# Second score products that begin with the row of maxima and end with the masks, on a TensorE that drops waits it has already made

## The chip, the cores and the metric

The kernel runs on 1 core of one Trainium2 chip. The metric is the device time in microseconds (us) of one execution. The kernel before takes 1175.02 us, the median of three runs (1172.75, 1175.02 and 1177.32).

## The reference

Everything is 32-bit. `x` is 4 sequences of 1024 tokens of width 128.

```
x = x + layernorm(attention(layernorm(x)))
x = x + layernorm(ffn(layernorm(x)))

attention(x): xn = layernorm(x) * g + b
    q, k, v = xn @ wq + bq, xn @ wk + bk, xn @ wv + bv      (16 heads of 64)
    scores = q @ k.T / 8;  scores[key < query] = -inf       (a query sees itself and what follows)
    out = softmax(scores) @ v @ w0 + b0 + x
ffn(x): down and up projections of 8 experts of rank 16, gated by the top 2 of the
    first token's logits
```

The inputs are drawn so that scores are large; a score must be right to nearly full 32-bit precision.

## The kernel before, in words

The work is cut into 32 slots of one pair of heads each (`t`, 4 sequences x 8 pairs), and each engine's program is written out slot by slot. A head has 64 rows, so every product of the pair is issued twice, head `h` on rows 0 to 63 and 64 to 127 of the array; the two run side by side, and a step of the array means such a pair here.

Scores are made twice. The **first** products, `score(n, s)` (S0 to S8, lines 519 to 529), have queries on partitions; they are single products `q_high x k_high`, and VectorE takes each row's maximum from them (L895, L890). GpSimd and a transpose (`m`) turn the maxima into the row `shift_row` of two bf16 parts. The **second** products, `score_t(n, s)` (T0 to T9, lines 531 to 558), have keys on partitions. Each tile of them is a sum in one PSUM bank per head of: three products of 32-bit operands (fp32r: `k_high x q_low`, `k_low x q_high`, `k_high x q_high`, L549), the row of maxima spread over the keys (`pick x shift_row`, bf16, L552), and, on the diagonal, four short bf16 products of 128 columns that add the mask (`mask_half x ident_half`, L556; in S tiles L527). ScalarE then takes the exponentials (L760) into `total` (T0 and T7) or a `ring` of five tiles. `weigh(n, s)` multiplies them with `v` (L571), and GpSimd adds them up (L417) for the sums of the softmax, which `sum_up` (L581) reduces over the partitions in the next slot.

A slot has three groups, each a string of S (first products of the slot ahead) and T (second products), then fills (`q`, `k`, `v` projections, L494 to L496 and L510 to L512, `out` L593, `sum` L581, `m` L587), then `weigh`:

```
ORDER = ["STTSTS", "STTSTTS", "STTSTS"]
T_STEPS = [range(0, 3), range(3, 7), range(7, 10)]
S_STEPS = [(1, range(3, 6)), (1, range(6, 9)), (2, range(0, 3))]
```

So TensorE's row is S3 T0 T1 S4 T2 S5, fills, weigh; S6 T3 T4 S7 T5 T6 S8, fill, weigh; S0 T7 T8 S1 T9 S2, fills, weigh. Masks end S1, S3, S6, S7, S8 and T4 to T9; T6 and T9 are two blocks each, of 384 and 128 columns, both with masks. T0 to T3 have none. T5 and T8 have 256 columns, the others 512.

Two PSUM banks, `st0` and `st1`, hold the T tiles in turn: T(s) waits for the exponential of T(s-2) (`s_exp`). There is one bank `s_ps` for the S tiles, so each S waits until VectorE has the maxima of the one before (`s_max`). Waits on TensorE are written where they are needed (`wait_ge`, `reach`, `wait_taken`), also where an earlier instruction of TensorE has already waited for the same or a later count.

Of the kernel before, what the change touches and what calls it, by code (L numbers as in the profile page):

```python
# [5 lines left out]
def sandwich_kernel(nc, x, ln_gb, w_pairs, qk_bias, bv, w0, b0, router_t, down_t, up_r, out, sums_dram):  # L6
# [102 lines left out]
    with ctx:  # L109
# [360 lines left out]

        @block.tensor
        def _(pe):
            def next_use(use):

                bank, index = USE[use]
                reach(pe, s_free[bank], index)

            def turn_four(src, a, bank=pp):
                for j in range(4):
# [3 lines left out]
            def project(weight, n):  # L483
                b, p = divmod(n, PAIRS)
                if b:
                    wait_taken(pe, "z", b, 0)
                else:
                    pe.wait_ge(s_xlow, 2)
                pe.wait_ge(s_w_low, 1 if p < 2 else 2)
                use = ("qk"[weight], n, 0)  # L490
                high, low = wqk_high[:, p, weight, :], wqk_low[:, p, weight, :]
                for c in range(2):
                    dst, tokens = at(*use)[:, c * HALF:(c + 1) * HALF], slice(c * HALF, (c + 1) * HALF)
                    nc.tensor.matmul(dst, high, x_low[:, tokens], start=True, stop=False)  # L494
                    nc.tensor.matmul(dst, low, x_high[:, tokens], start=False, stop=False)  # L495
                    last = nc.tensor.matmul(dst, high, x_high[:, tokens], start=False, stop=True)  # L496
                return last

            def project_v(n, part):
                b, p = divmod(2 * n, PAIRS)  # L500
                if b:
                    wait_taken(pe, "z", b, 0)
                else:
                    pe.wait_ge(s_xlow, 2)
                pe.wait_ge(s_w_low, 1 if p < 2 else 2)
                high, low = (w[:, p:p + 2, :].rearrange("p a c -> p (a c)") for w in (wv_high, wv_low))
                for a in range(4):
                    t = 4 * part + a
                    dst, tokens = at("v", n, part)[:, a * 2 * P:(a + 1) * 2 * P], slice(t * P, (t + 1) * P)
                    nc.tensor.matmul(dst, x_low[:, tokens], high, start=True, stop=False)  # L510
                    nc.tensor.matmul(dst, x_high[:, tokens], low, start=False, stop=False)
                    last = nc.tensor.matmul(dst, x_high[:, tokens], high, start=False, stop=True)  # L512
                return last

            def score(n, s):

                if s == 0:
                    pe.wait_ge(s_high, 2 * n + 2)
                reach(pe, s_max, BLOCK_STEPS * n + s)
                rows = [slice(h * D, (h + 1) * D) for h in range(2)]  # L520
                for i, k0, w, col, diagonal in BLOCKS[s]:
                    for h in range(2):
                        last = nc.tensor.matmul(s_ps[:, h, col:col + w], q_high[n % 3][rows[h], i * P:(i + 1) * P],  # L523
                                                k_high[n % 3][rows[h], k0:k0 + w], start=True, stop=not diagonal)
                    for a in range(2 * diagonal):
                        for h in range(2):
                            last = nc.tensor.matmul(s_ps[:, h, col:col + P], ident_half[rows[h], a, :],  # L527
                                                    mask_half[rows[h], a, :], start=False, stop=(a == 1))
                last.then_inc(s_score, 1)

            def score_t(n, s):

                half = half_of(s)
                if s == 0:
                    wait_taken(pe, "k", n, 0)
                if s == 0:
                    pe.wait_ge(s_shift_row, 32 * n + 32)
                reach(pe, s_exp, STEPS * n + s - 1)
                g = 0 if s < 3 else 1 if s < 7 else 2
                reach(pe, s_free[s % 2], filled[n, g][s % 2])  # L540
                rows = [slice(h * D, (h + 1) * D) for h in range(2)]
                b = n % 3
                for _, j, w, col in TILES[s]:
                    keys, queries = slice(j * P, (j + 1) * P), slice(half * HALF, half * HALF + w)
                    dst = [st[s % 2][:, h, col:col + w] for h in range(2)]
                    diagonal = j // 4 == half
                    for k, q in ((k_high[b], q_low[b]), (k_low[b], q_high[b]), (k_high[b], q_high[b])):
                        for h in range(2):
                            nc.tensor.matmul(dst[h], k[rows[h], keys], q[rows[h], queries], start=(q is q_low[b]),  # L549
                                             stop=False)  # L550
                    for h in range(2):
                        last = nc.tensor.matmul(dst[h], pick[rows[h], :], shift_row[n % 2][rows[h], queries], start=False,  # L552
                                                stop=not diagonal)
                    for a in range(2 * diagonal):
                        for h in range(2):
                            last = nc.tensor.matmul(dst[h][:, w - P:w], mask_half[rows[h], a, :],  # L556
                                                    ident_half[rows[h], a, :], start=False, stop=(a == 1))
                last.then_inc(s_st, 1)

            def weigh(n, s):  # L560

                half = half_of(s)
                pe.wait_ge(s_exp, STEPS * n + s + 1)
                if s in FIRST:
                    reach(pe, s_o, 2 * n + half)
                if s == 0:
                    wait_taken(pe, "v", n // 2, 1)
                for k, (_, j, w, col) in enumerate(TILES[s]):
                    for h in range(2):
                        c0 = (n % 2) * P + h * D  # L570
# [3 lines left out]
                last.then_inc(s_pv, 1)  # L574

            def sum_up(n):
                pe.wait_ge(s_add, SUMS * (n + 1))
                for half in range(2):
                    for h in range(2):
                        g = 2 * half + h  # L580
# [2 lines left out]
                return last  # L583

            def turn_shift(n):
                pe.wait_ge(s_shift, n + 1)
                return nc.tensor.transpose(pp[:].bitcast(bf16)[0:32, 0:P], shift[:].rearrange("p h s i -> p (h s i)"),  # L587
                                           ident_bf[:])

            def project_out(n):  # L590
                pe.wait_ge(s_norm, n + 1)
                for t in range(QB):
                    last = nc.tensor.matmul(at("out", n, 0)[:, t * P:(t + 1) * P], o_norm[:, t * P:(t + 1) * P],  # L593
                                            w0_sb[:, n % PAIRS, :], start=True, stop=True)
# [9 lines left out]
            def fill(use, bank):  # L604
# [11 lines left out]
                elif kind == "out":  # L616
                    last = project_out(n)
                elif kind == "c0":
                    pe.wait_ge(s_bvw, 1)
                    for p in range(PAIRS):  # L620
                        last = nc.tensor.matmul(dst[:, 0:E], bv_wide[:, p, :], w0_sb[:, p, :], start=(p == 0),
                                                stop=(p == PAIRS - 1))
                elif kind == "z":
                    pe.wait_ge(s_z, n + 1)
                    for a in range(2):
                        last = turn_four(z_a, a, dst[:, a * HALF:(a + 1) * HALF])
                elif kind == "u":
                    pe.wait_ge(s_u, n + 1)
                    for a in range(2):
                        last = turn_four(u_b, a, dst[:, a * HALF:(a + 1) * HALF])  # L630
                elif kind == "logit":
                    pe.wait_ge(s_first, n + 1)
                    last = nc.tensor.matmul(dst[:, 0:EXPERTS], first_tok[:], router_sb[:], start=True, stop=True)
                elif kind == "down":
                    wait_taken(pe, "u", n, 0)
                    for a in range(2):
                        half = slice(a * HALF, (a + 1) * HALF)
                        last = nc.tensor.matmul(dst[:, half], down_sb[:], u_t[:, half], start=True, stop=True)
                elif kind == "up":
                    wait_taken(pe, "down", n, 0)  # L640
                    pe.wait_ge(s_upg, n + 1)
                    for a in range(2):
                        last = project_up(dg_t, a, dst[:, a * HALF:(a + 1) * HALF])
                last.then_inc(s_fill[bank], 1)

            pe.wait_ge(s_const, 5)
            pe.wait_ge(s_small, 16 * 8)
            pe.wait_ge(s_z0, 1)
            turn_four(z_a, 0, st[0][:, 0, :]).then_inc(s_zt, 1)
            pe.wait_ge(s_z, 1)  # L650
            turn_four(z_a, 1, st[0][:, 1, :]).then_inc(s_xt, 1)

            for t in SLOTS:
                for g in range(3):
# [7 lines left out]
                            score_t(t, s)  # L662
                    for use, bank in fills(t, g):
                        if bank != "pp" and 0 <= t < N:
                            pe.wait_ge(s_exp, STEPS * t + T_STEPS[g][-1] + (bank == T_STEPS[g][-1] % 2))
                        fill(use, bank)
                    if 0 <= t < N:
                        for s in T_STEPS[g]:
                            weigh(t, s)

            b = B - 1
            pe.wait_ge(s_u, B)
            turn_four(u_b, 0, st[0][:, 0, :])
            turn_four(u_b, 1, st[0][:, 1, :]).then_inc(s_tail, 1)
            pe.wait_ge(s_first, B)
            nc.tensor.matmul(pp[:, 0:EXPERTS], first_tok[:], router_sb[:], start=True, stop=True).then_inc(s_tail, 1)
            pe.wait_ge(s_ut_out, 2)
            for a in range(2):
                last = nc.tensor.matmul(st[1][:, a, :], down_sb[:], u_t[:, a * 512:(a + 1) * 512], start=True, stop=True)
            last.then_inc(s_tail, 1)  # L680
            pe.wait_ge(s_dg, 2)
            pe.wait_ge(s_upg, B)
            for a in range(2):
                last = project_up(dg_t, a, s_ps[:, a, :])
            last.then_inc(s_tail, 1)
# [422 lines left out]
```

## Time and profile before

| | us |
|---|---|
| median of three runs | 1175.02 |
| the profiled execution | 1177.26 |
| its span, first to last instruction | 1175.5 |
| TensorE (PE) busy | 1048.6 (89%) |
| GpSimd (POOL) busy | 746.3 (63%) |
| VectorE (DVE) busy | 546.3 (46%) |
| ScalarE (ACT) busy | 541.7 (46%) |
| granted TensorE clock, mean | 0.957 |

Busy times are unions of an engine's records; PE is the matmuls, PEld the loads of their stationary operand, which may run beside a matmul. A matmul's record includes the time until its result is written, so records of neighbours overlap; the distance from start to start tells what a step costs. A steady slot is 31.2 us long.

### The profile page before, as it was taken

How to read it: one execution, taken by the hardware profiler on the slowest of the kernel's cores; microseconds unless marked ns; L12 is line 12 of the kernel's file. 1: busy time of each engine (PE TensorE's matmuls, PEld its weight loads, DVE VectorE, ACT ScalarE, POOL GpSimd, SP SyncE). 2: the span in 40 equal slices, each digit the busy share in tenths (PEclk: the TensorE clock that was granted, in tenths of full speed). 3: DMA queues.
4: the chain of work that ended last, by engine and by line, in shares of the span. 5: the costliest groups of instructions: out<-in, count | busy, mean ns of one | idle time of the engine just before them, and what ended most of it. 6: DMA issues, size and time to landing. Idle time of an engine off the chain costs nothing.

```text
span 1175.5 us, 22750 instructions
## 1 busy us (share of the span) xinstructions
PE 1048.6 (89%) x9160; PEld 648.2 (55%) x9160; DVE 546.3 (46%) x748; ACT 541.7 (46%) x738; POOL 746.3 (63%) x681
## 2 busy tenths in 40 slices
PE   0679999999999998999999998999999999999513
PEld 0345655665666665666655665666565656655312
DVE  1345455455445544455545554555555545452012
ACT  3124554444444564554454553654454454543212
POOL 8006768666666866765776866766776766765531
PEclk9979999999999998999999998999999999999855
DMA  3000000001001000001002100000002000000010
GB/s 97 0 19 3 20 20 20 20 20 38 20 21 25 19 16 20 20 20 38 20 20 56 20 19 2 21 20 20 20 20 56 20 20 20 12 14 16 19 54 18
DMA packets 63174, 27.62 MB, mean 23 GB/s; under 512 B 40160, under 2 KB 54880, under 8 KB 63072
## 3 DMA queue, kind: packets, MB, share of 16 engines
q1 hardware_dynamic: 63072, 26.18, 9.6%
q8 instruction: 74, 1.21, 0.4%
q14 instruction: 28, 0.23, 0.1%
HBM read 23.28 MB, written 2.36 MB: 22 GB/s over the span
## 4 chain that ended last, share of the span: by engine, by line
PE 74%; POOL 10%; ACT 7%; DVE 5%; issue 3%; DMA 1%; POOLq 0%; SPq 0%; ACTq 0%; DVEq 0%
PE po L571 20%; PE st L549 14%; PE s_ps L523 7%; PE st L593 5%; POOL total L417 5%; PE st L552 4%; PE st L494 4%; DVE least L895 4%; ACT ring L760 3%; PE pp L581 3%; PE st L496 3%; PE st L495 3%; ACT total L760 3%; PE s_ps L527 2%; PE st L510 2%
## 5 line engine op out<-in xcount | busy, mean ns | idle before, releaser
L417 POOL TENSOR_TENSOR total<-total,ring 128x1024 f32<-128x1024 f32 (+3 forms) x320 | 549.2, 1716 | 325.4 <-PE po L571 292.7
L895 DVE TENSOR_REDUCE least<-s_ps 128x2 f32<-128x1024 f32 (+2 forms) x320 | 317.9, 1010 | 316.4 <-PE s_ps L527 207.7
L760 ACT ACTIVATE ring<-st 128x1024 f32<-128x1024 f32 (+1 forms) x256 | 234.8, 918 | 227.0 <-PE st L552 152.7
L571 PE MATMUL po<-ring,v_sb 128*64 128x512 f32 (+3 forms) x1280 | 210.7, 467 | 0.0
L523 PE MATMUL s_ps<-k_high,q_high 64*128 64x512 f32 (+3 forms) x768 | 165.1, 442 | 21.1 <-DVE least L895 15.9
L549 PE MATMUL st<-q_low,k_high 64*128 64x512 f32 (+3 forms) x768 | 168.2, 434 | 5.2 <-ACT total L760 1.1
L571 PEld LDWEIGHTS po<-ring,v_sb 128*64 128x64 f32 x1280 | 89.0, 137 | 135.4 <-issue 125.7
L549 PE MATMUL st<-q_high,k_low 64*128 64x512 f32 (+3 forms) x768 | 133.3, 343 | 0.0
L549 PE MATMUL st<-q_high,k_high 64*128 64x512 f32 (+3 forms) x768 | 133.1, 342 | 0.0
L552 PE MATMUL st<-shift_row,pick 64*128 64x512 bf16 (+3 forms) x768 | 129.6, 333 | 0.0
L523 PEld LDWEIGHTS s_ps<-k_high,q_high 64*128 64x128 f32 x768 | 74.5, 190 | 71.2 <-issue 36.5
L760 ACT ACTIVATE total<-st 128x1024 f32<-128x1024 f32 x64 | 65.6, 1025 | 61.5 <-PE st L552 34.8
L549 PEld LDWEIGHTS st<-q_low,k_high 64*128 64x128 f32 x768 | 73.5, 187 | 29.2 <-ACT total L760 19.8
L424 POOL TENSOR_TENSOR o_norm<-o_raw,inv_row 128x1024 f32<-128x1024 f32 x32 | 75.8, 2368 | 14.7 <-DMA inv_row<-sums_dram 14.7
L942 DVE SCALAR_TENSOR_TENSOR q_low<-st,bias_col,q_high 128x1024 fp32r<-128x1024 f32 x32 | 41.1, 1284 | 85.3 <-ACT q_high L788 85.3
L766 ACT COPY o_raw<-po 128x512 f32<-128x512 f32 x64 | 37.4, 584 | 91.4 <-PE po L571 91.2
L593 PE MATMUL st<-w_sb,o_norm 128*128 128x128 f32 x512 | 67.5, 289 | 11.5 <-POOL o_norm L424 11.4
L549 PEld LDWEIGHTS st<-q_high,k_high 64*128 64x128 f32 x768 | 72.5, 185 | 8.4
L593 PEld LDWEIGHTS st<-w_sb,o_norm 128*128 128x128 f32 x512 | 66.8, 205 | 17.8 <-issue 13.3
L549 PEld LDWEIGHTS st<-q_high,k_low 64*128 64x128 f32 x768 | 73.3, 187 | 2.9
L552 PEld LDWEIGHTS st<-shift_row,pick 64*128 64x128 bf16 x768 | 37.2, 93 | 65.6 <-issue 62.8
L527 PE MATMUL s_ps<-mask_half,ident_half 64*128 64x128 bf16 x1024 | 71.8, 224 | 0.0
(133 smaller groups left out, 1325.9 us busy)
## 6 DMA issues: line engine op xcount, KB each, us to landing
inv_row<-sums_dram SPq DMA_DIRECT2D x64, 256.0 KB, 4.0
x_a<-x SPq DMA_DIRECT2D x4, 512.0 KB, 4.7
sums<-sums_row SPq DMA_DIRECT2D x128, 2.0 KB, 2.1
x_b<-x SPq DMA_DIRECT2D x4, 512.0 KB, 5.7
out<-res_b SPq DMA_DIRECT2D x4, 512.0 KB, 4.1
ring<-w_pairs SPq DMA_DIRECT2D x1, 1152.0 KB, 8.4
shift_row<-shift_t SPq DMA_DIRECT2D x64, 4.0 KB
w_sb<-w SPq DMA_DIRECT2D x1, 512.0 KB, 5.3
```

Source lines behind the costliest of these rows:

```text
L417: nc.gpsimd.tensor_tensor(so_far, so_far, tile_of(n, s)[:, :, col:col + w], ALU.add).then_inc(s_add, 1)
L424: nc.gpsimd.tensor_tensor(o_norm[:], o_raw[n % 2][:], inv_row[:], ALU.mult).then_inc(s_norm, 1)
L494: nc.tensor.matmul(dst, high, x_low[:, tokens], start=True, stop=False)
L523: last = nc.tensor.matmul(s_ps[:, h, col:col + w], q_high[n % 3][rows[h], i * P:(i + 1) * P], k_high[n % 3][rows[h], k0:k0 + w], start=Tru ...
L527: last = nc.tensor.matmul(s_ps[:, h, col:col + P], ident_half[rows[h], a, :], mask_half[rows[h], a, :], start=False, stop=(a == 1))
L549: nc.tensor.matmul(dst[h], k[rows[h], keys], q[rows[h], queries], start=(q is q_low[b]), stop=False)
L552: last = nc.tensor.matmul(dst[h], pick[rows[h], :], shift_row[n % 2][rows[h], queries], start=False, stop=not diagonal)
L571: last = nc.tensor.matmul(po[h * D:(h + 1) * D, 0:w], v_sb[(n // 2) % 2][:, j, c0:c0 + D], tile_of(n, s)[:, h, col:col + w], start=(s in F ...
L593: last = nc.tensor.matmul(at("out", n, 0)[:, t * P:(t + 1) * P], o_norm[:, t * P:(t + 1) * P], w0_sb[:, n % PAIRS, :], start=True, stop=True)
L760: nc.scalar.activation(tile_of(n, s)[:, :, 0:w], st[s % 2][:, :, 0:w], ACT.Exp, scale=SCALE).then_inc(s_exp, 1)
L895: last = nc.vector.tensor_reduce(least[:, :, a:a + 1], s_ps[:, :, col:col + w], AX.X, ALU.max, negate=True)
L942: nc.vector.scalar_tensor_tensor(out=low[n % 3][:], in0=src, scalar=bias_col[:, n % PAIRS, w:w + 1], in1=high[n % 3][:].bitcast(fp32), op0 ...
```

## The change

Two edits, both in TensorE's program. In `score_t`, each tile begins with the row of maxima and then takes its three 32-bit products, the two small ones in the other order; the masks, where there are some, follow the last 32-bit product. And TensorE keeps, per semaphore, the highest count it has waited for (`made`); `need` emits a wait only where the count is higher. All waits of TensorE go through it. Other engines are not touched.

```diff
+            made = {}
+
+            def need(semaphore, count):
+
+                if count > made.get(semaphore, 0):
+                    made[semaphore] = count
+                    pe.wait_ge(semaphore, count)
+
+            def need_taken(*use):
+                bank, index = USE[use]
+                need(s_free[bank], index + 1)
...
-                    for k, q in ((k_high[b], q_low[b]), (k_low[b], q_high[b]), (k_high[b], q_high[b])):
+                    for h in range(2):
+                        nc.tensor.matmul(dst[h], pick[rows[h], :], shift_row[n % 2][rows[h], queries], start=True, stop=False)
+                    for part, (k, q) in enumerate(((k_low[b], q_high[b]), (k_high[b], q_low[b]), (k_high[b], q_high[b]))):
                         for h in range(2):
-                            nc.tensor.matmul(dst[h], k[rows[h], keys], q[rows[h], queries], start=(q is q_low[b]),
-                                             stop=False)
-                    for h in range(2):
-                        last = nc.tensor.matmul(dst[h], pick[rows[h], :], shift_row[n % 2][rows[h], queries], start=False,
-                                                stop=not diagonal)
+                            last = nc.tensor.matmul(dst[h], k[rows[h], keys], q[rows[h], queries], start=False,
+                                                    stop=(part == 2 and not diagonal))
                     for a in range(2 * diagonal):
...
             def weigh(n, s):
 
                 half = half_of(s)
-                pe.wait_ge(s_exp, STEPS * n + s + 1)
+                need(s_exp, STEPS * n + s + 1)
                 if s in FIRST:
-                    reach(pe, s_o, 2 * n + half)
+                    need(s_o, 2 * n + half)
```

Every other `wait_ge`, `reach` and `wait_taken` of TensorE becomes `need` or `need_taken` in the same way. In the built program TensorE's instructions that do nothing but wait go from 749 to 174, and matmuls that carry a wait from 1142 to 883; the 7956 matmuls stay.

TensorE's row in the second group of a slot, where S6 ends and T3 begins, before (names are output<-moving operand, stationary operand; columns of the output at the end):

```order
L523 MATMUL s_ps<-k_high,q_high 128x256 x2
L527 MATMUL s_ps<-mask_half,ident_half 128x128 x4
L549 MATMUL st<-q_low,k_high 128x512 [waits s_free_1,s_exp]
L549 MATMUL st<-q_low,k_high 128x512
L549 MATMUL st<-q_high,k_low 128x512 x2
L549 MATMUL st<-q_high,k_high 128x512 x2
L552 MATMUL st<-shift_row,pick 128x512 x2
```

The same place now:

```order
L535 MATMUL s_ps<-k_high,q_high 128x256 x2
L539 MATMUL s_ps<-mask_half,ident_half 128x128 x4
L560 MATMUL st<-shift_row,pick 128x512 [waits s_free_1]
L560 MATMUL st<-shift_row,pick 128x512
L563 MATMUL st<-q_high,k_low 128x512 x2
L563 MATMUL st<-q_low,k_high 128x512 x2
L563 MATMUL st<-q_high,k_high 128x512 x2
```

A bf16 product now stands behind the bf16 masks, and the wait for `s_exp` is gone from it, since an earlier one covers it.

TensorE's row a little later in the same group, where T6 begins behind T5's masks, before:

```order
L556 MATMUL st<-ident_half,mask_half 128x128 x4
L549 MATMUL st<-q_low,k_high 128x384 [waits s_free_0,s_exp]
L549 MATMUL st<-q_low,k_high 128x384
L549 MATMUL st<-q_high,k_low 128x384 x2
L549 MATMUL st<-q_high,k_high 128x384 x2
L552 MATMUL st<-shift_row,pick 128x384 x2
L556 MATMUL st<-ident_half,mask_half 128x128 x4
```

And now:

```order
L567 MATMUL st<-ident_half,mask_half 128x128 x4
L560 MATMUL st<-shift_row,pick 128x384 [waits s_exp]
L560 MATMUL st<-shift_row,pick 128x384
L563 MATMUL st<-q_high,k_low 128x384 x2
L563 MATMUL st<-q_low,k_high 128x384 x2
L563 MATMUL st<-q_high,k_high 128x384 x2
L567 MATMUL st<-ident_half,mask_half 128x128 x4
```

The wait for the exponential stays and now holds the bf16 product; the masks follow a 32-bit product instead of a bf16 one.

## Rows read from the trace of the kernel before

**Rows 1.** The page: shares of the chain that ended last, by engine.

```profile
PE 74%; POOL 10%; ACT 7%; DVE 5%; issue 3%; DMA 1%; POOLq 0%; SPq 0%; ACTq 0%; DVEq 0%
```

**Rows 2.** The chain in a steady slot: start us, us, engine, output, line.

```profile
605.03 1.03 ACT ring L760
606.07 0.04 issue
606.11 0.79 PE st L549 x6
...
614.57 1.03 ACT total L760
...
615.65 0.79 PE st L549 x6
...
624.55 1.24 DVE least L895
...
637.30 0.80 PE st L549 x6
```

**Rows 3.** Timeline, S6's masks and T3: start us, us, engine, line, operation.

```profile
602.68 0.29 PE L527 MATMUL s_ps<-mask_half,ident_half 64*128 64x128 bf16 x4
...
603.09 0.39 PE L549 MATMUL st<-q_high,k_low 64*128 64x512 f32 x2
...
603.32 0.40 PE L549 MATMUL st<-q_high,k_high 64*128 64x512 f32 x2
...
603.56 0.20 PEld L549 LDWEIGHTS st<-q_low,k_high 64*128 64x128 f32 x2
...
603.79 0.19 PEld L549 LDWEIGHTS st<-q_high,k_low 64*128 64x128 f32 x2
```

**Rows 4.** Timeline, T4's masks, S7, S7's masks, T5.

```profile
604.71 0.28 PE L556 MATMUL st<-ident_half,mask_half 64*128 64x128 bf16 x4
...
604.80 0.48 PE L523 MATMUL s_ps<-k_high,q_high 64*128 64x512 f32 x2
...
605.12 0.29 PE L527 MATMUL s_ps<-mask_half,ident_half 64*128 64x128 bf16 x4
...
605.22 0.36 PE L549 MATMUL st<-q_low,k_high 64*128 64x256 f32 x2
```

**Rows 5.** Timeline, T6 from its wait on: loads and masks.

```profile
606.11 0.19 PEld L549 LDWEIGHTS st<-q_low,k_high 64*128 64x128 f32 x2 [0.23 <-ACT ring L760]
...
606.22 0.19 PEld L549 LDWEIGHTS st<-q_high,k_low 64*128 64x128 f32 x2
...
606.92 0.28 PE L556 MATMUL st<-ident_half,mask_half 64*128 64x128 bf16 x4
606.98 0.19 PEld L549 LDWEIGHTS st<-q_low,k_high 64*128 64x128 f32 x2
...
607.09 0.19 PEld L549 LDWEIGHTS st<-q_high,k_low 64*128 64x128 f32 x2
...
607.37 0.10 PEld L552 LDWEIGHTS st<-shift_row,pick 64*128 64x128 bf16 x2
...
607.38 0.15 PEld L556 LDWEIGHTS st<-ident_half,mask_half 64*128 64x128 bf16 x4
```

**Rows 6.** Timeline, steps of 512 columns before `out`, and before weigh.

```profile
597.32 0.39 PE L496 MATMUL st<-x_high,wqk_high 128*128 128x512 f32 x1
597.55 0.72 PE L593 MATMUL st<-w_sb,o_norm 128*128 128x128 f32 x5
```

**Rows 7.** Timeline, the end of the `k` fill and the first product of weigh.

```profile
609.50 0.40 PE L496 MATMUL st<-x_high,wqk_high 128*128 128x512 f32 x1
609.83 2.37 PE L571 MATMUL po<-ring,v_sb 128*64 128x512 f32 x12
```

**Rows 8.** Waits of TensorE (us, times, longest), and one slot's busy times and clock.

```profile
PE pp L581 <- POOL total L417: 18.0, 4, 8.9
...
723.80:757.90 34.10, 33.80 (x284) 20.70 (x285) 14.05 (x15) 18.39 (x29) 23.19 (x23) 0.91 0.08 18
```

More of the change, by code:

```diff
@@ L472, in _ @@
         def _(pe):
+            made = {}
[6 more added lines that the diff above has]
+                need(s_free[bank], index + 1)
             def next_use(use):
                 bank, index = USE[use]
-                reach(pe, s_free[bank], index)
+                need(s_free[bank], index)
             def turn_four(src, a, bank=pp):
@@ L485, in project @@
                 if b:
-                    wait_taken(pe, "z", b, 0)
+                    need_taken("z", b, 0)
                 else:
-                    pe.wait_ge(s_xlow, 2)
-                pe.wait_ge(s_w_low, 1 if p < 2 else 2)
+                    need(s_xlow, 2)
+                need(s_w_low, 1 if p < 2 else 2)
                 use = ("qk"[weight], n, 0)
@@ L501, in project_v @@
                 if b:
-                    wait_taken(pe, "z", b, 0)
+                    need_taken("z", b, 0)
                 else:
-                    pe.wait_ge(s_xlow, 2)
-                pe.wait_ge(s_w_low, 1 if p < 2 else 2)
+                    need(s_xlow, 2)
+                need(s_w_low, 1 if p < 2 else 2)
                 high, low = (w[:, p:p + 2, :].rearrange("p a c -> p (a c)") for w in (wv_high, wv_low))
@@ L517, in score @@
                 if s == 0:
-                    pe.wait_ge(s_high, 2 * n + 2)
-                reach(pe, s_max, BLOCK_STEPS * n + s)
+                    need(s_high, 2 * n + 2)
+                need(s_max, BLOCK_STEPS * n + s)
                 rows = [slice(h * D, (h + 1) * D) for h in range(2)]
@@ L534, in score_t @@
                 if s == 0:
-                    wait_taken(pe, "k", n, 0)
+                    need_taken("k", n, 0)
                 if s == 0:
-                    pe.wait_ge(s_shift_row, 32 * n + 32)
-                reach(pe, s_exp, STEPS * n + s - 1)
+                    need(s_shift_row, 32 * n + 32)
+                need(s_exp, STEPS * n + s - 1)
                 g = 0 if s < 3 else 1 if s < 7 else 2
-                reach(pe, s_free[s % 2], filled[n, g][s % 2])
+                need(s_free[s % 2], filled[n, g][s % 2])
                 rows = [slice(h * D, (h + 1) * D) for h in range(2)]
@@ L562, in weigh @@
                 half = half_of(s)
-                pe.wait_ge(s_exp, STEPS * n + s + 1)
+                need(s_exp, STEPS * n + s + 1)
                 if s in FIRST:
-                    reach(pe, s_o, 2 * n + half)
+                    need(s_o, 2 * n + half)
                 if s == 0:
-                    wait_taken(pe, "v", n // 2, 1)
+                    need_taken("v", n // 2, 1)
                 for k, (_, j, w, col) in enumerate(TILES[s]):
@@ L576, in sum_up @@
             def sum_up(n):
-                pe.wait_ge(s_add, SUMS * (n + 1))
+                need(s_add, SUMS * (n + 1))
                 for half in range(2):
@@ L585, in turn_shift @@
             def turn_shift(n):
-                pe.wait_ge(s_shift, n + 1)
+                need(s_shift, n + 1)
                 return nc.tensor.transpose(pp[:].bitcast(bf16)[0:32, 0:P], shift[:].rearrange("p h s i -> p (h s i)"),
@@ L590, in project_out @@
             def project_out(n):
-                pe.wait_ge(s_norm, n + 1)
+                need(s_norm, n + 1)
                 for t in range(QB):
@@ L618, in fill @@
                 elif kind == "c0":
-                    pe.wait_ge(s_bvw, 1)
+                    need(s_bvw, 1)
                     for p in range(PAIRS):
@@ L623, in fill @@
                 elif kind == "z":
-                    pe.wait_ge(s_z, n + 1)
+                    need(s_z, n + 1)
                     for a in range(2):
@@ L627, in fill @@
                 elif kind == "u":
-                    pe.wait_ge(s_u, n + 1)
+                    need(s_u, n + 1)
                     for a in range(2):
@@ L631, in fill @@
                 elif kind == "logit":
-                    pe.wait_ge(s_first, n + 1)
+                    need(s_first, n + 1)
                     last = nc.tensor.matmul(dst[:, 0:EXPERTS], first_tok[:], router_sb[:], start=True, stop=True)
                 elif kind == "down":
-                    wait_taken(pe, "u", n, 0)
+                    need_taken("u", n, 0)
                     for a in range(2):
@@ L639, in fill @@
                 elif kind == "up":
-                    wait_taken(pe, "down", n, 0)
-                    pe.wait_ge(s_upg, n + 1)
+                    need_taken("down", n, 0)
+                    need(s_upg, n + 1)
                     for a in range(2):
@@ L644, in fill @@
                 last.then_inc(s_fill[bank], 1)
-            pe.wait_ge(s_const, 5)
-            pe.wait_ge(s_small, 16 * 8)
-            pe.wait_ge(s_z0, 1)
+            need(s_const, 5)
+            need(s_small, 16 * 8)
+            need(s_z0, 1)
             turn_four(z_a, 0, st[0][:, 0, :]).then_inc(s_zt, 1)
-            pe.wait_ge(s_z, 1)
+            need(s_z, 1)
             turn_four(z_a, 1, st[0][:, 1, :]).then_inc(s_xt, 1)
@@ L664, in _ @@
                         if bank != "pp" and 0 <= t < N:
-                            pe.wait_ge(s_exp, STEPS * t + T_STEPS[g][-1] + (bank == T_STEPS[g][-1] % 2))
+                            need(s_exp, STEPS * t + T_STEPS[g][-1] + (bank == T_STEPS[g][-1] % 2))
                         fill(use, bank)
@@ L671, in _ @@
             b = B - 1
-            pe.wait_ge(s_u, B)
+            need(s_u, B)
             turn_four(u_b, 0, st[0][:, 0, :])
             turn_four(u_b, 1, st[0][:, 1, :]).then_inc(s_tail, 1)
-            pe.wait_ge(s_first, B)
+            need(s_first, B)
             nc.tensor.matmul(pp[:, 0:EXPERTS], first_tok[:], router_sb[:], start=True, stop=True).then_inc(s_tail, 1)
-            pe.wait_ge(s_ut_out, 2)
+            need(s_ut_out, 2)
             for a in range(2):
@@ L680, in _ @@
             last.then_inc(s_tail, 1)
-            pe.wait_ge(s_dg, 2)
-            pe.wait_ge(s_upg, B)
+            need(s_dg, 2)
+            need(s_upg, B)
             for a in range(2):
```

## The prediction

> **What bounds the kernel now.** I read the page's chain of waits first, then the chain inside one steady slot, then the timeline of TensorE there, start by start. The chain is three quarters TensorE, with short pieces of the others in it [rows 1]. A steady slot takes 31.19 us, from T6's start at 606.11 to the next T6's at 637.30 [rows 2]. In it TensorE is stopped at four places, and three of them are on the chain: T6 waits for the exponential of T4, which ends at 606.06; T9 waits for that of T7, which ends at 615.60; and S5 waits for VectorE's maxima of S4 (624.55 and 1.24 us) [rows 2]. The fourth is T2, between S4 and S5, and the maxima cover it. So four stretches set the slot: from S5 to S4's end, S4 to S5 through VectorE, S5 on to T4's end (its exponential releases T6), and T6 to T7's end (its exponential releases T9). What TensorE saves in T5, between T4 and T6, in T8, between T7 and T9, or in T2 only lengthens a stall.
>
> What the timeline shows is when a load of the stationary operand is hidden. The second load behind T3's masks tells it: a step of 512 columns takes 0.23 us (603.09 to 603.32), but from the masks' start to T3's second product 0.41 pass [rows 3]. A pair of masks takes 0.06 (606.92 to 606.98), and the 32-bit load that starts with the last pair needs 0.11 until the array is handed over (606.98 to 607.09) [rows 5]. The last pair is 0.06 long, so 0.05 to 0.06 is bare. Behind a step of 256 columns or more the same load is hidden. Where TensorE had stopped, the whole 0.11 is bare (606.11 to 606.22), while a bf16 load hands over after 0.01 (607.37 to 607.38) [rows 5].
>
> **The change, part by part.** Steps are pairs of heads.
>
> 1. *T0 and T3 now begin with the bf16 product behind the masks of S3 and S6.* Before, the load of `k_high` is bare for 0.055. Now the load of `pick` is short and lies under the last mask pair, and the load of `k_low` starts with the product of 512 columns that hides it: the load of T4's `k_high` did so in T3 (603.56, while the bf16 step lasts until 603.79) [rows 3]. The 0.01 that the first bf16 load costs behind a 32-bit step is also gone. Gain 0.065 each, say 0.13 in a slot. Both lie on the chain.
>
> 2. *T6 and T9 begin with the bf16 product after their stall.* The bare load shrinks from 0.11 to 0.01; the load of `k_low` then lies under 384 columns. Gain 0.10 each. The bounds are 0.10 and, if a bf16 load in an idle array took all of its own record of 0.10 [rows 5], nothing. I take 0.10: the hand-over is what counted for the 32-bit load too, whose record is 0.19 and whose cost is 0.11.
>
> 3. *T5 and T8 gain as T0 does*, about 0.06, ahead of the stalls of T6 (0.23 us, [rows 5]) and of T9. Worth nothing; if those stalls were gone it would be worth 0.12 a slot. The second blocks of T6 and T9 (128 columns) gain nothing: the 32-bit load that was bare behind the masks is now bare behind the equally short bf16 product.
>
> 4. *Masks now follow a 32-bit product.* In S7 they do already: from masks to the next step 0.10 (605.12 to 605.22), against 0.09 in T4 behind a bf16 product (604.71 to 604.80) [rows 4]. Cost 0.01 for each diagonal block. T4 and T7 moreover are entered from a 32-bit step without having gained, another 0.01. T4 and T7 end 0.02 later each, and so do the exponentials that release T6 and T9; T6's and T9's two blocks give 0.01 net (the narrow bf16 step in front of the masks was already 0.01 long). So minus 0.02 and 0.01 at both places, 0.06 in a slot.
>
> 5. *The swap of the two small 32-bit products* moves nothing: both operands are ready a slot ahead, both loads are alike. What used to be last in T0 to T3 was a bf16 step, now a 32-bit one; their records are 0.39 and 0.40, 0.01 at most until ScalarE starts.
>
> 6. *The dropped waits.* 575 instructions that only wait are gone, 18 in a slot. They were all for counts that were reached long before. Their cost is bounded by two places. Before `out` (L593), three semaphores are waited for, and the step before it takes 0.23 as any other (597.32 to 597.55) [rows 6]; so nothing. Before weigh the step takes 0.33 (609.50 to 609.83) [rows 7], 0.10 more, and there the wait and a change of the array's shape (128 x 128 to 128 x 64) fall together; so 0.10 at one place in a slot, 3 us in all, if it is the wait. I take 0, since at `out` three waits come together and the shape stays, and nothing is lost. What hides them is the step that runs while the waits are read; without that cover each would cost its own reading time wherever TensorE has just stopped.
>
> Sum for a steady slot: 0.13 + 0.20 - 0.06 = 0.27 us. It does not count everywhere. Four times `sum_up` waits for GpSimd, 18.0 us in all [rows 8], and GpSimd holds 10% of the chain [rows 1], 118 us, close to a whole slot each time. In those four slots T3, T6 and T9 are off the chain and only about 0.07 is left. 28 x 0.27 + 4 x 0.07 = 7.8 us. The start, before the first slot, and the tail have no T tile.
>
> Against the profiled execution's own 1177.26 this gives 1169.5. That run was 2.2 above the median; the median 1175.02 becomes 1167.2.
>
> The load of a bf16 operand has a price on a page too. The Trainium skill, TensorE: Matmul & The Clock Gate, Weight-path perf modes, says of the fast weight load that it is measured at about twice the speed of a 32-bit one. By that an idle array would take half of 0.11, the gain of part 2 would be 0.05 each and the sum some 3 us smaller, an estimate; the trace's 0.01 speaks for more, though it stands behind a running step and not behind a stall.
>
> **The rivals.**
>
> *A, the waits cost as well.* If the 0.10 before weigh is the wait, the third group of each slot (the `k` fill, where the first weigh product now has no wait) gains 0.10, and perhaps two more fills as much. 3 to 9 us more: 1158 to 1164. For it: the surplus of 0.10 stands in front of a waiting product [rows 7]. Against: `out` [rows 6].
>
> *B, no change.* The array needs every load somewhere, the bare one only moves: from behind the masks to behind the bf16 step. Then the time stays within 2 us of 1175. Against it: the load under way during a bf16 step of 512 columns [rows 3]. The Trainium skill, TensorE: Matmul & The Clock Gate, What overlaps and what doesn't, has a rule that would make it so: a load overlaps a running matmul only if it goes to other rows of the array. By that rule each head's load would be bare in either order and the change would be worth nothing. This trace disagrees: 0.19 of load and 0.23 of product on the same rows fit into 0.23 [rows 3].
>
> *C, partial.* The stalls take more than I think: GpSimd's stretches reach further, or T6 is released by the exponential of T3 and T4 in a row and not by T4's end alone, so that T3's gain counts and part of the rest doesn't; or the bf16 load after a stall costs 0.05. 3 to 5 us: 1170 to 1172.
>
> *D, slower.* The masks behind a 32-bit product wait for their load. S7 shows 0.01, but there the bank was not being added to by a wide chain. Six of the eight such blocks are on the chain (T4, T7 and both blocks of T6 and of T9). If each had its full load record of 0.10 bare, the slot would lose 6 x 0.09 = 0.54 and win 0.33, minus 0.2, or 6 us slower: 1181. It decides from about 0.055 per block. Against: every L527 after L523 in the trace has 0.01 [rows 4].
>
> Besides these the clock: after a long stop of TensorE the granted clock is at half (1.2 GHz) for some us; the slot behind one such stop took 34.1 us at a mean of 0.91 [rows 8], fills of its own included. Where GpSimd is waited for, a faster TensorE stops longer. One more stretch at half clock costs up to 3 us.
>
> **How the numbers follow.** Forecast 0.60, A 0.12, B 0.10, C 0.14, D 0.04. A measurement of this kernel tells about 0.5%, 5.9 us, from no change; "faster" is thus below 1169.1. Most of the forecast's mass (0.60, whose own spread is about 1164.5 to 1170.5 with the runs' scatter of 2 us) and all of A lie there: 0.51 + 0.12 and 0.03 of C, 0.66. Slower is D, 0.03. The rest, 0.31, is within 0.5%. The range reaches down into A to 1162 and up through C and into B to 1174.
>
> **What would show it.** In the profile after: from the start of S6's last masks to T3's second product 0.34 instead of 0.41; after the stall of T6 the next load starts 0.01 and not 0.11 behind; the masks of T tiles 0.10 long; a steady slot of 30.9 us; TensorE's stalls at T6 and T9 longer, by 0.05; and the 0.10 before weigh still there. If a steady slot is still 31.19, B holds; if the step before weigh falls to 0.23, A; if the loads of the masks stand bare by 0.05 or more, D. An answer above 1174 or below 1162 makes the prediction wrong.

## The result and the profile after

| | before | changed |
|---|---|---|
| median, us | 1175.37 (1172.75 to 1177.32, 4 runs) | 1162.49 (1161.46 to 1164.02, 4 runs) |
| profiled execution, us | 1177.26 | 1162.28 |
| its span, us | 1175.5 | 1160.5 |
| granted clock, mean | 0.957 | 0.959 |

The ratio is 0.9893, with a 95% interval of 0.987 to 0.9915: 1.1% faster. The forecast was 1167.2 in a range of 1162 to 1174; the time is inside it, 0.5 above its lower end, and the gain of 12.9 us is 1.65 times the 7.8 that the sum gave.

The page of the changed kernel, the chain's shares by engine and TensorE's group that now stands at the head of each tile:

```profile
PE 74%; POOL 9%; ACT 7%; DVE 5%; issue 2%; DMA 1%; SPq 0%; POOLq 0%; ACTq 0%; DVEq 0%
...
L560 PE MATMUL st<-shift_row,pick 64*128 64x512 bf16 (+3 forms) x768 | 127.4, 328 | 9.3 <-ACT total L771 1.2
```

The limits are the same as in [rows 1]. The chain in the steady slots (start us, us, engine, output, line) answers to [rows 2]:

```profile
629.51 1.03 ACT ring L771
638.98 1.03 ACT total L771
648.80 1.24 DVE least L906
660.44 1.03 ACT ring L771
```

The same three waits stand on the chain, and the slot, from one exponential of T4 to the next, is 30.93 us long. In the kernel before it was 31.22, by the same kind of row at 636.23 and 667.45:

```profile
636.23 1.03 ACT ring L760
667.45 1.03 ACT ring L760
```

The timeline of the changed kernel at T3 shows the load that is hidden now (compare [rows 3]). L539 are S6's masks, L560 the row of maxima, L563 the 32-bit products:

```profile
658.14 0.28 PE L539 MATMUL s_ps<-mask_half,ident_half 64*128 64x128 bf16 x4
658.21 0.10 PEld L560 LDWEIGHTS st<-shift_row,pick 64*128 64x128 bf16 x2
...
658.27 0.19 PEld L563 LDWEIGHTS st<-q_high,k_low 64*128 64x128 f32 x2
...
658.48 0.19 PEld L563 LDWEIGHTS st<-q_low,k_high 64*128 64x128 f32 x2
```

The first bf16 load starts with the last mask pair (658.21), and the array is handed over 0.06 later (658.27, where the next load starts). The second product takes the array where the load behind it starts, at 658.48: 0.34 after the masks' start instead of 0.41. At T6, after the stall (compare [rows 5]):

```profile
661.52 0.10 PEld L560 LDWEIGHTS st<-shift_row,pick 64*128 64x128 bf16 x2 [0.29 <-ACT ring L771]
...
661.53 0.20 PEld L563 LDWEIGHTS st<-q_high,k_low 64*128 64x128 f32 x2
...
661.70 0.19 PEld L563 LDWEIGHTS st<-q_low,k_high 64*128 64x128 f32 x2
```

The bf16 load hands over after 0.01 here too, where before the 32-bit one took 0.11, and the load of `k_low` is under way during the step of 384 columns (661.53 to 661.70). TensorE's idle time in front grew from 0.23 to 0.29, as it should with T5's gain lying ahead of it. And the step before weigh, with no wait left between it and the first product of weigh, against [rows 7]:

```profile
664.84 0.39 PE L508 MATMUL st<-x_high,wqk_high 128*128 128x512 f32 x1
665.15 0.65 PE L582 MATMUL po<-ring,v_sb 128*64 128x512 f32 x2
```

It still takes 0.31. Over all 25 places where the `k` fill stands before weigh, the median step is 0.326 before, 0.318 in the changed kernel and 0.318 in the run below that has the new order with all the old waits. So the surplus over 0.23 isn't the wait.

**Where the rest came from.** The two spans differ by 15.0 us. Taken from each slot's `sum_up` to the next, the 31 slots between the first and the last give 11.3, the start before them 1.5 and the tail 2.1. Twenty-eight of the slots give 6.3 us together: the plain ones 0.26 to 0.32 each, those with additional fills 0.13 to 0.27, and the four in which GpSimd is waited for nothing. The other three give 5.0: the slots that begin at 206.5, 723.7 and 1045.2 in the trace before give 1.89, 0.97 and 2.18. In them the granted clock differs. Busy times, then the granted clock (third column from the right), before, for the stretch behind the stop at 206.5 and for the third of these slots, around 1068:

```profile
206.00:214.00 8.00, 7.47 (x38) 5.09 (x40) 2.69 (x3) 3.23 (x6) 0.68 (x2) 0.79 0.03 1
1060.00:1092.00 32.00, 29.99 (x245) 17.75 (x243) 5.63 (x16) 12.49 (x17) 19.76 (x13) 0.95 0.08 18
```

The same stretches of the program in the changed kernel:

```profile
204.00:212.00 8.00, 7.58 (x50) 4.39 (x50) 2.42 (x2) 3.24 (x6) 2.27 (x2) 1.00 0.03 1
1048.00:1080.00 32.00, 29.79 (x263) 16.96 (x261) 6.92 (x18) 13.50 (x18) 21.90 (x15) 1.00 0.12 27
```

A clock of 0.79 over 8 us is 3.4 us at half (1.2 GHz), and 0.95 over 32 is about as much. In the slot that begins at 723.7 the mean clock is 0.91 before [rows 8] and 0.93 in the changed kernel:

```profile
716.50:749.70 33.20, 32.67 (x284) 20.16 (x285) 13.97 (x15) 18.44 (x29) 23.22 (x23) 0.93 0.08 18
```

At the first of these places TensorE had stopped for 1.51 us before and for 1.85 in the changed kernel.

Most of the 1.5 us at the start is not the change's. The first T tile starts at 78.76 before and at 77.62 in the changed kernel, so 1.1 us are gained before any edited tile has run; only the stretch that gives the other 0.4 holds T tiles (those of the first slot). Nor can the tail's 2.1 be put down to it: the tail has no T tile, and it lasts 69.2 to 69.5 us in the three traces of the kernel before, 67.1 in this trace of the changed kernel (mean clock 0.60), and 69.5 in its second trace (0.57).

### The profile page after: what moved, and what is told of

It is laid out like the page before. It is cut to its first block, busy times and chain, and to the rows that moved or that the text cites. A ratio compares the mean times of both kernels' runs of the same rounds, so it can differ in the third digit from the quotient of the medians.

```text
span 1160.5 us, 22175 instructions
## 1 busy us (share of the span) xinstructions
PE 1024.6 (88%) x9160; PEld 641.8 (55%) x9160; DVE 547.0 (47%) x748; ACT 541.0 (47%) x738; POOL 746.6 (64%) x681
## 4 chain that ended last, share of the span: by engine, by line
PE 74%; POOL 9%; ACT 7%; DVE 5%; issue 2%; DMA 1%; SPq 0%; POOLq 0%; ACTq 0%; DVEq 0%
PE po L582 21%; PE st L563 13%; PE s_ps L535 7%; PE st L604 5%; PE st L560 5%; POOL total L417 4%; PE st L506 4%; DVE least L906 4%; ACT ring L771 3%; PE pp L592 3%; PE st L507 3%; ACT total L771 3%; PE st L508 3%; PE st L567 2%; PE s_ps L539 2%
## 5 line engine op out<-in xcount | busy, mean ns | idle before, releaser
L563 PE MATMUL st<-q_high,k_low 64*128 64x512 f32 (+3 forms) x768 | 185.0, 478 | 0.0
L535 PE MATMUL s_ps<-k_high,q_high 64*128 64x512 f32 (+3 forms) x768 | 159.4, 427 | 23.7 <-DVE least L906 18.9
L560 PE MATMUL st<-shift_row,pick 64*128 64x512 bf16 (+3 forms) x768 | 127.4, 328 | 9.3 <-ACT total L771 1.2
L563 PE MATMUL st<-q_high,k_high 64*128 64x512 f32 (+3 forms) x768 | 133.0, 342 | 0.0
L563 PE MATMUL st<-q_low,k_high 64*128 64x512 f32 (+3 forms) x768 | 132.5, 341 | 0.0
L563 PEld LDWEIGHTS st<-q_high,k_high 64*128 64x128 f32 x768 | 72.3, 185 | 8.2
L563 PEld LDWEIGHTS st<-q_low,k_high 64*128 64x128 f32 x768 | 73.4, 187 | 4.8
L563 PEld LDWEIGHTS st<-q_high,k_low 64*128 64x128 f32 x768 | 75.3, 192 | 0.0
L567 PE MATMUL st<-ident_half,mask_half 64*128 64x128 bf16 x1024 | 73.4, 221 | 0.0
L539 PE MATMUL s_ps<-mask_half,ident_half 64*128 64x128 bf16 x1024 | 71.7, 224 | 0.0
```

The source lines that it names most:

```text
L563: last = nc.tensor.matmul(dst[h], k[rows[h], keys], q[rows[h], queries], start=False, stop=(part == 2 and not diagonal))
```

## The experiments

### The order alone

The kernel before with the new body of `score_t`, all waits left as they were: 749 instructions that only wait.

```diff
-                    for k, q in ((k_high[b], q_low[b]), (k_low[b], q_high[b]), (k_high[b], q_high[b])):
...
+                        nc.tensor.matmul(dst[h], pick[rows[h], :], shift_row[n % 2][rows[h], queries], start=True, stop=False)
+                    for part, (k, q) in enumerate(((k_low[b], q_high[b]), (k_high[b], q_low[b]), (k_high[b], q_high[b]))):
```

> The new order inside score_t with all the old waits. Theory (waits cost nothing, the order gives 0.28 us in a steady slot, and what the result has beyond 8 us came from where the half-clock stretches fell): 8 to 12 us below before, steady slot 30.92 us as in the changed kernel. Rival (the dropped waits gave the 4 to 5 us that the order doesn't explain): no more than 8 us below before, and 4 to 5 us above the changed kernel.

1163.62 us (1161.67 to 1165.38, 6 runs) against 1174.18 for the kernel before on the same chip (18 runs); ratio 0.9911, 0.9891 to 0.9931. The slot, by the chain:

```profile
629.43 1.03 ACT ring L759
660.32 1.03 ACT ring L759
```

30.89 us. The order alone gives the whole slot, and it lies 10.6 us below the kernel before, in the 8 to 12 expected; a contribution of the waits of 4 to 5 us falls.

### The waits alone

The changed kernel with the old body of `score_t`.

> The old order inside score_t with the waits dropped as in the change. Theory: no difference from before, within 2 us, steady slot 31.2 us. Rival: 4 to 5 us below before.

1175.64 us (1170.61 to 1177.16, 12 runs), ratio to the kernel before 1.0004, 0.9987 to 1.002. The slot is as before:

```profile
636.26 1.03 ACT ring L772
667.49 1.03 ACT ring L772
```

The dropped waits are worth nothing that can be measured here.

### More waits

```diff
                 need(s_free[s % 2], filled[n, g][s % 2])
+                for _ in range(4):
+                    pe.wait_ge(s_const, 5)
```

> The changed kernel with four waits more at the head of each second score tile, for a count reached at the start of the kernel: 640 instructions more that only wait, 814 in all against 749 before the change. Theory: nothing, within 2 us of the changed kernel, steady slot 30.92. Rival (each costs its own record of 0.05 us where TensorE has just been stopped or is short of work): up to 0.1 us per stalled tile, 0.3 per slot, 8 us above the changed kernel.

The four waits of a tile make two instructions of two waits each. 1162.93 us (1162.48 to 1165.53, 6 runs), the changed kernel's time. With 640 waiting instructions more, twenty in a slot, the slot stays at 30.93:

```profile
629.69 1.03 ACT ring L773
660.62 1.03 ACT ring L773
```

Adding waits shows what removing them did: a satisfied wait costs TensorE nothing where a step runs while it is read. The rival, a cost where TensorE has just been stopped, is not tested by it. At T6 the added waits stand ahead of the wait that stops TensorE, and the trace has their records at 660.69 and 660.80, while the stop ends at 661.70. So what a wait costs that is read behind a stop stays open.

### T0 and T3 alone

```diff
-                    for h in range(2):
-                        nc.tensor.matmul(dst[h], pick[rows[h], :], ...
...
+                    if s in (0, 3):
...
+                    else:
...
```

The branch holds the new order, the `else` the old one.

> The changed kernel, with the new order in tiles T0 and T3 alone (those behind masks that no stall follows); the others have the old order. Theory: 0.13 us less per slot than before, steady slot 31.06, some 4 us below before. Rival (the load of k_high behind masks was not bare): steady slot 31.2.

1167.61 us (1166.57 to 1168.87, 6 runs), 6.6 below the kernel before (some 4 expected); ratio 0.9943, 0.9922 to 0.9965. The slot:

```profile
633.17 1.03 ACT ring L780
664.22 1.03 ACT ring L780
```

31.05 us, 0.17 less than 31.22, where 0.13 had been expected: the load behind the masks was bare. The two tiles give 0.04 more than the expected 0.13, and no run says where that comes from.

### T6 and T9 alone

The same edit with `s in (6, 9) and col == 0`.

> The changed kernel, with the new order in the first block of T6 and of T9 alone (those that begin after a stall). Theory: the 32-bit load of 0.11 us in an idle array becomes a bf16 load of 0.01; less about 0.01 for the masks, so 0.17 to 0.19 us per slot, steady slot 31.02, some 5 us below before. Rival (a bf16 load in an idle array costs 0.05 or its whole record of 0.10): 0.10 or 0 per slot, steady slot 31.1 or 31.2.

1168.29 us (1167.34 to 1169.9, 7 runs), 5.9 below the kernel before (some 5 expected); ratio 0.9955, 0.9936 to 0.9974. The slot:

```profile
633.28 1.03 ACT ring L780
664.35 1.03 ACT ring L780
```

31.07, 0.15 less. That lies between the theory's 0.17 to 0.19 and the rival's 0.10. The load itself is settled by the timeline above, 0.01; where the shortfall of 0.02 to 0.04 comes from was not shown. Together with the run before it, the two halves give 0.32, against 0.29 for the whole change. The tiles in neither half that can cost time are T4 and T7, as part 4 of the prediction has it. The timelines agree for T7: the whole of T6 takes 0.10 less (606.11 to 607.50 before, 661.52 to 662.81 now), but from T6's start to T9's, with T7 in between, only 0.07 is left (9.54 before, 9.47 now). No run had T4 and T7 alone.

### T5 and T8 alone

The same edit with `s in (5, 8)`.

> The changed kernel, with the new order in T5 and T8 alone, whose gain lies ahead of a stall. Theory: nothing, steady slot 31.2, the time of before within 2 us (T6's and T9's stalls grow by 0.05). Rival (the stalls are not what they seem, and TensorE's own work sets the slot): 0.12 less per slot, 31.08, 3 to 4 us below before.

1175.49 us (1170.66 to 1176.5, 12 runs); ratio to the kernel before 1.0017, 1.0002 to 1.0031. The slot:

```profile
633.89 1.03 ACT ring L780
665.12 1.03 ACT ring L780
```

31.23: no gain, as a saving ahead of a stall should give. The median is 3.3 us above that of the kernel before beside it (1172.17, 17 runs), where 2 had been the bound; the slots don't show these 3.3 us, and both kernels scatter by some 6 us.

### The masks second

```diff
+                    for a in range(2 * diagonal):
+                        for h in range(2):
+                            nc.tensor.matmul(dst[h][:, w - P:w], mask_half[rows[h], a, :],
+                                             ident_half[rows[h], a, :], start=False, stop=False)
                     for part, (k, q) in enumerate(((k_low[b], q_high[b]), (k_high[b], q_low[b]), (k_high[b], q_high[b]))):
```

> The changed kernel, but each tile's masks directly behind the bf16 row, before the three 32-bit products. Theory: the load of k_low is bare behind the masks (0.055 per block), the load of the S tile that follows is not any more. T4 and T7 end 0.04 to 0.05 later and T6 and T9 start so much later; inside T6 and T9 both effects cancel. Steady slot 31.01 to 31.03, some 3 us above the changed kernel. Rival (bf16 products together are best, a switch of operand type is what costs): steady slot 30.85 or less, faster than the changed kernel.

1167.45 us (1165.14 to 1168.4, 6 runs), 5.0 above the changed kernel, where some 3 had been expected. The slot:

```profile
631.75 1.03 ACT ring L771
662.79 1.03 ACT ring L771
```

31.04, where 31.01 to 31.03 had been expected. The 31 slots together are 2.3 us longer than the changed kernel's in the two traces; the other 3 us lie in the start and the tail, where that kernel's own two traces differ by 1.0 and 2.4. The timeline shows the bare load in its new place, T6's masks (L563) and the products behind them (L567):

```profile
664.04 0.28 PE L563 MATMUL st<-ident_half,mask_half 64*128 64x128 bf16 x4
664.12 0.42 PE L567 MATMUL st<-q_high,k_low 64*128 64x384 f32 x2
664.38 0.33 PE L567 MATMUL st<-q_low,k_high 64*128 64x384 f32 x2
664.55 0.34 PE L567 MATMUL st<-q_high,k_high 64*128 64x384 f32 x2
```

From the masks' start to the second product 0.34 pass, of which the masks are 0.11 and the step 0.17; 0.06 is bare. Grouping the bf16 products this way costs time; what counts is which load stands behind the short step.

### Both blocks' products first, then all masks

The version that the reading points to. In the tiles with two blocks (S3, S6, S8, T6, T9) the products of both come first; the narrow block's bf16 product goes ahead of the wide one's, so that the wide one hides the 32-bit load. Only the first product of a bank starts it.

```diff
-                for _, j, w, col in TILES[s]:
...
+                for place, (_, queries, dst, _, _) in enumerate(blocks[::-1]):
+                    for h in range(2):
+                        nc.tensor.matmul(dst[h], pick[rows[h], :], shift_row[n % 2][rows[h], queries], start=(place == 0),
+                                         stop=False)
+                for part, (k, q) in enumerate(((k_low[b], q_high[b]), (k_high[b], q_low[b]), (k_high[b], q_high[b]))):
+                    for keys, queries, dst, _, diagonal in blocks:
...
+                for _, _, dst, w, diagonal in blocks:
+                    for a in range(2 * diagonal):
```

> A version meant to be faster, built on what the trace taught: where a tile has two blocks in one bank (S3, S6, S8, T6, T9), the products of both blocks come first and all their masks last, so that no 32-bit load follows a mask or the narrow bf16 product inside a tile. Theory: in S3, S6 and S8 one bare load of 0.055 us and one switch of 0.01 less each, in T6 and T9 one bare load and about 0.02 each, 0.33 to 0.35 per slot on the chain: steady slot 30.6, some 9 us below the changed kernel, 1153 to 1155. Rival (the bare loads are a fixed price that moves elsewhere, B of the prediction): steady slot 30.9, 1162.

1156.98 us (1155.84 to 1159.3, 4 runs); ratio to the kernel before 0.9865, 0.9844 to 0.9887. It is the fastest of all. The slot:

```profile
626.32 1.04 ACT ring L779
656.88 1.03 ACT ring L779
```

30.56 us, 0.37 less than the changed kernel's 30.93, a little over the 0.33 to 0.35 expected. But 1153 to 1155 had been expected, and the median is only 5.5 below the changed kernel and not 9. In this trace the stretch behind the first stop for GpSimd is at half clock for most of its 8 us:

```profile
202.00:210.00 8.00, 7.74 (x34) 5.13 (x36) 1.76 (x2) 3.24 (x6) 0.11 (x1) 0.61 0.03 1
```

TensorE had stopped there for 2.20 us, against 1.85 in the changed kernel. The slot behind this stop is 33.36 us long instead of 30.95, which takes 2.4 us back; the other thirty give 8.6 together, as the forecast of 9 had it. The start gives 1.5 more, and the tail, 69.2 instead of 67.1, takes 2.1.

### The kernels themselves, once more

No edit. Of the 18 times of the kernel before beside the order-only run, 9 are from 1170.59 to 1173.23 and 9 from 1175.12 to 1177.48, with nothing in between. The 17 beside the later experiments, on another chip, don't part so: 11 are from 1170.69 to 1172.44, 4 from 1173.38 to 1174.86, and the other two 1175.95 and 1177.27.

> The kernel before, unchanged, once more for its trace. Its times so far lie in two clusters, near 1171.5 and near 1176. Theory (which of them a run falls into is where the stretches at half clock fall): steady slot 31.21 in any run; a run near 1171 has shorter slots in one or two of the places where the first trace had a half-clock stretch (the slot of 32.81 after the stop at 206.5, and the one of 31.98 at 1068). Rival: all slots shorter by 0.1.

> The same as the run before it, for a second trace of the kernel before.

> The changed kernel, unchanged, once more for its trace. Theory: steady slot 30.92, and the same two places free of half-clock stretches or nearly so, 1161 to 1165. Rival (the changed kernel has them as often as before): a run near 1167.

The two traces of the kernel before came out at 1177.41 and 1173.01 us, the changed kernel's at 1163.81. The first has all its slots within 0.1 of the trace that the prediction was read from. The slot of the 1173.01 run is 31.18, that of the changed kernel's 30.90:

```profile
634.96 1.04 ACT ring L760
666.14 1.04 ACT ring L760
```

```profile
628.51 1.03 ACT ring L771
659.41 1.03 ACT ring L771
```

What sets the 1173.01 run apart is in the slots with a change of clock. In the 1173.01 run, the slot behind the stop at 723 is 32.62 long instead of 34.12, the one near 1068 30.33 instead of 31.98, and the one behind 462 is 32.75 instead of 33.29: 3.7 of the 4.2 us between its span of 1171.3 and the first trace's 1175.5. The stretch near 206 is at half clock in it too (0.79), the one near 1068 is not (1.00):

```profile
205.50:213.50 8.00, 7.63 (x38) 4.92 (x40) 2.50 (x3) 3.23 (x6) 0.72 (x2) 0.79 0.03 1
1056.00:1088.00 32.00, 29.98 (x255) 16.76 (x255) 6.74 (x18) 12.88 (x17) 21.36 (x15) 1.00 0.12 26
```

So the theory came true at one of its two places, near 1068, and not at the other. The slot at 206 is 32.8 long in all three traces of the kernel before, and 30.9 in both of the changed kernel and in those with the order alone and with more waits. That can't be put down to shorter slots alone, since the run with only T5 and T8 in the new order, whose slots are as long as before, also has the full clock there, after the same stop of 1.5 us:

```profile
206.00:214.00 8.00, 7.75 (x56) 4.53 (x56) 2.42 (x2) 3.23 (x6) 2.26 (x2) 1.00 0.03 1
```

## Why the prediction was right, and where it wasn't

*What bounds the kernel, and the slot.* Right, and this is what the experiments show to be the cause: the order alone gives the slot, the waits alone don't. A slot of 30.92 had been expected and 30.93 was found, with the same three waits on the chain.

*Part 1 (T0, T3).* Right in kind, 0.13 forecast and 0.17 measured alone. *Part 2 (T6, T9).* Right in kind; 0.20 forecast before the loss of the masks, 0.15 measured with it. The 0.01 in an idle array held (661.52 to 661.53 in the timeline). The Trainium skill (TensorE: Matmul & The Clock Gate, Weight-path perf modes) has the fast load at about twice the speed; the records agree with that, 0.10 against 0.19 us. But the price in the row is the time until the array is handed over, 0.01 against 0.11, and the 0.05 that the prediction worked out from the factor did not come. *Part 3 (T5, T8).* Right, 0. *Part 4 (the masks behind a 32-bit product).* Right in size as far as seen: the sum of the two halves exceeds the whole by 0.03, and the timelines have it at T7. *Part 5.* The swap was not tried by itself. *Part 6 (the waits).* Right that they are worth nothing, by removal and by addition. That each would cost its own reading time behind a stop is shown by no run.

*What was off is the step from the slot to the whole.* "28 x 0.27 + 4 x 0.07 = 7.8 us" is close to what the tile order gives: 6.3 in the slots where the clock is alike in both traces, 0.2 to 0.3 for each of the other three, and at most 0.4 for the tiles of the first slot, so 7.1 to 7.5. It errs a little in two ways that nearly cancel: the plain slots give a trifle more than 0.27, those with additional fills 0.13 to 0.27, and GpSimd's four 0, not 0.07. The two traces differ by 15.0 us. Of the other 7.5, some 4 are in the three slots with a different clock, 1.1 in the start before any edited tile, and 2.1 in the tail. The prediction put the start and the tail at nothing, and the clock only on the side of loss.

The tile order alone, by these slots, would have given about 1167.5, the forecast's number. That the time stayed inside the range with the rest added is luck. The forecast's own spread was 1164.5 to 1170.5, and 1162.49 lies below it; the lower bound of 1162 stood there for rival A, in whose 1158 to 1164 the time falls, and A is false. The forecast subtracted from three runs of which two were among the slower half of what this kernel does: from the lower group on one chip, whose middle is 1171.1, to 1162.5 there are 8.6 us, from the upper one 13.4, and on the chip of the later experiments the changed kernel with more waits is 9.2 below the kernel before. The changed kernel's five runs spread by 2.6 us, too few to say that it has no second group. Why its stops fall so that less of the work behind them is at half clock is left open.

*The rivals.* A fell with the waits alone, the added waits, and the step before weigh. B fell: the kernel with the tile order alone is 10.6 us faster, with 0.33 of it in each steady slot. The rule of the Trainium skill (TensorE: Matmul & The Clock Gate, What overlaps and what doesn't), that a load overlaps a product only on other rows of the array, is contradicted by the load of `k_low` at 661.53, which lasts 0.20 and lies within the bf16 product on the same rows, 661.52 to 661.86. C fell: the gain of T0 and T3 and that of T6 and T9 both count, and the bf16 load costs 0.01; only GpSimd's four slots give less than expected, 0.3 us in all. D fell: T4's masks are loaded at 660.11 and start at 660.12, so their load costs 0.01 behind a 32-bit product.

## What to carry to other kernels

In a row of matmuls, look at what follows each short one. Here a 32-bit stationary operand (64 x 128) hands the array over 0.11 us after its load starts, and if the step before it lasts 0.06 the rest is bare; a bf16 operand of that size hands it over after 0.01. Put short bf16 products in front of other bf16 products or of a wide step, begin with one after a stall, and gather the short ones of several blocks at the end of the tile. Waits that are already satisfied and read while a step runs need not be removed from TensorE's program for time's sake. A forecast from one trace should first say which stretches of it were at half clock, and a gain should be read from the steady slots and not from the whole time alone.

## What the runs showed of the hardware that was not expected

- 640 waiting instructions more on TensorE, each 0.05 us in its record and all satisfied, cost nothing: a slot of 30.93 us with and without them.
- A load of a 32-bit operand of 64 x 128 has a record of 0.19 us and holds the array back for 0.11; one in bf16 has 0.10 and holds it back for 0.01.
- Behind a stop of TensorE of 1.5 us the clock was at half in the three traces of the kernel before and at full in the run with T5 and T8 alone; behind one of 1.85 us it was at full in the changed kernel; behind one of 2.20 us it was at 0.61 over 8 us. So the length of the stop doesn't decide it by itself.
- On one chip the kernel before has two groups of times with middles 4.8 us apart (1171.1 and 1175.9, 18 runs), on another the gap is filled (17 runs), while its steady slots agree within 0.04 us (31.18 and 31.22).
